# Output projection of six batches as three fp32r terms, with a per-tile split and single-buffered exponentials, in an RWKV + MoE layer

## The chip, the cores and the metric

The kernel runs on one core of one Trainium2 chip. The time is the device time of one launch in microseconds (us); less is better. Five engines work side by side: TensorE (PE, with its weight load PEld), VectorE (DVE), ScalarE (ACT), GpSimd (POOL) and the DMA queue that SyncE (SP) issues.

## The reference

For x of 8 batches x 512 steps x 512 channels (float32):

```python
shifted = pad(x)[:, :-1]
k = (x*mk + shifted*(1-mk)) @ Wk;  v = (... mv) @ Wv;  r = sigmoid((... mr) @ Wr)
# per channel, over time: a decaying, max-stabilised softmax average of v under weights exp(k)
out_t = (e1*num + e2*v_t) / (e1*den + e2);  num, den, mx updated with the decay
x = layernorm(x + (r * out) @ Wo)                   # the "output projection" is @ Wo
x = layernorm(x + moe(x))                           # 8 experts of 16 units, top 2, silu
```

## The kernel before

Channels lie on the 128 partitions in C = 4 chunks, time on the free axis. The unit of the recurrence is one chunk of one batch, 128 channels x 512 steps, U = 32 units. Every engine runs the same hand-written loop over **slots** s = 0..31; slot s works on unit u = s of batch b = s // 4, and j = s % 4 is its place in the batch. No scheduler moves anything: each engine does its list in program order and waits on semaphores.

In slot s:

- TensorE computes the key of unit s+1 (`key`, PSUM bank PK0 or PK1), the receptance of unit s (`rec`, bank PR) and the value of unit s+1 (`value`, bank PV). From batch 1 on each is a `split`: weights and inputs are stored as a high part (rounded to fp32r) and a low part (the rest), and every product is three fp32r matmuls (high x high, high x low, low x high), 12 per unit. Batch 0 uses plain fp32 (`whole`).
- VectorE runs the recurrence: `scan_den`, `value_kept`, `scan_num`, `value_now`, `numerator`, then `scan_max` and `lead` for unit s+1, `gate`, `weigh`. `weigh` writes r * out of the unit to a ring RW. It also makes the token-shift mixes of the next batch (`mix`: 4 chunks for each of key, value, receptance; it reads D and XT, both in SBUF), and the two residuals.
- ScalarE forms the exponentials (`decay_gates`: three Relus; `decay_exps`: three Exps, both into EX), the sigmoid chain on PR (`receptance`, `log_g`, `factor`), the high parts of the mixes (`highs`) and the layernorm spreads.
- GpSimd forms the denominators (`denominator`: DQ from DEN and EX), the low parts of the mixes (`lows`: mix minus high part; KL in slots j = 2, VL and RL in slots j = 3), the layernorm scaling (`normalise`), and in slots j = 0 the four differences D of the next batch.

The ring through the engines in one slot is: `lead` (DVE) -> `decay_gates` (ACT) -> `log_g`, `factor` (ACT) -> `weigh` (DVE) -> ... -> `scan_den` of the next slot. `gate` (DVE) has to be done before `log_g`, and it waits for the receptance's Exps.

The output projection of a batch runs four slots later: tile t (128 time steps) in slot t + 4 for t < 24 and two tiles in each of slots 28 and 29. It is `project(t)`: four fp32 matmuls of 512 columns into bank PP, stationary operand 128 x 128 columns of RW, moving operand WO. In slots j = 0 it stands before `rec`, else after `rec` and the transposes `turn`. The last four tiles (28 to 31) are done in the tail.

Buffers that matter here: EX is two buffers (EX[u % 2]), RW a ring of 8 units, KT four separate mix buffers, SCR a scratch of 4 chunks that holds the key mixes of batch 0 and the throw-away output of the layernorm squares. Wk, Wv and Wr are staged in X1T, XN0 and XN1, then split into high and low parts in slots 0 to 2; a low part of 128x2048 is made on VectorE for Wk (`WKL`) and on GpSimd for Wv and Wr (`WVL`, `WRL`).

Of the kernel before, what the change touches and what calls it, by code (L numbers as in the profile page):

```python
# [23 lines left out]
NRW = 8  # L24
# [5 lines left out]
def rwkv_moe_postln(nc, x, xt, vec, wk, wv, wr, wo, dr, up, tri, out):  # L30
    with ExitStack() as ctx:
# [13 lines left out]
        WO = sb("WO", [128, C, H])  # L45
# [10 lines left out]
        KT = [sb(f"KT{i}", [128, T]) for i in range(NKT)]  # L56
# [52 lines left out]
        class Part:  # L109
            def __init__(self, k):  # L110
# [7 lines left out]
                self.s1, self.s2 = (x[:, i, EI * lo:EI * hi] for i in range(2))  # L118
                self.gt, self.eq = (x[:, 2 if tail else 1, o + E * E * lo:o + E * E * hi] for o in (0, 256))
# [82 lines left out]
        def _(eng):  # L202
# [66 lines left out]
        def _(eng):  # L269
# [844 lines left out]
```

## Time and profile before

| | |
|---|---|
| time, 3 runs | 499.42 us median (499.01 to 499.54) |
| the profiled execution | 498.65 us, its span 496.8 us |
| PE busy | 471.4 us (95%) |
| DVE busy | 409.2 us (82%) |
| ACT busy | 339.9 us (68%) |
| POOL busy | 259.7 us (52%) |
| granted TensorE clock | 0.99 of full speed over the span |

A batch repeats every 57.4 us from batch 3 on: the `scan_den` of slots 17 to 21 start at 247.09, 260.31, 273.63, 290.21 and 304.45 us. Busy time of an engine says how full it is, not whether anybody waits for it; for that the timelines show in brackets the idle time before an instruction and what ended it. "x4" in a timeline row means four instructions merged, and an fp32 matmul of 512 columns appears as two records.

### The profile page before, as it was taken

The page shows a single profiled execution, that of the slowest core. Times are in us where ns is not written, and L with a number is a line of the kernel's source. Part 1 is how long each engine was busy: PE and PEld are TensorE (multiplying, and loading weights), DVE is VectorE, ACT ScalarE, POOL GpSimd, SP SyncE. Part 2 cuts the span into 40 slices and gives each one's busy share as a digit, 9 for nine tenths or more (in the row PEclk, how much of TensorE's full clock was granted, in tenths as well). Part 3 has the DMA queues.
Part 4 walks back from the last instruction along what each step waited for, and adds up shares of the span by engine and source line. Part 5 has one row for each costly group of instructions (what it writes and reads, how often), then busy time and mean ns, then how long its engine had stood idle before and what let it go on. Part 6 is the DMA issues. An engine that isn't in the chain of part 4 may idle for free. (4 is left out here: it accounts for less than half of the span.)

```text
span 496.8 us, 6301 instructions
## 1 busy us (share of the span) xinstructions
PE 471.4 (95%) x1850; PEld 315.1 (63%) x1850; DVE 409.2 (82%) x655; ACT 339.9 (68%) x769; POOL 259.7 (52%) x279
## 2 busy tenths in 40 slices
PE   8998799999999999999999999999999998989991
PEld 3444367776776666766867666776767666756550
DVE  6998988897799869997799887997799977755686
ACT  1568465766877587777877768776877776936574
POOL 2446763666425973556815965358625664021226
PEclk9999899999999999999999999999999999999997
DMA  9800340002000232003210043003120013300005
GB/s 249 275 8 5 126 146 1 0 11 77 1 1 0 72 99 85 1 1 128 74 53 1 22 128 106 0 1 114 58 84 1 0 43 107 106 0 2 1 35 220
DMA packets 20098, 30.35 MB, mean 61 GB/s; under 512 B 2016, under 2 KB 7136, under 8 KB 20064
## 3 DMA queue, kind: packets, MB, share of 16 engines
q1 hardware_dynamic: 20064, 29.95, 18.6%
q8 instruction: 15, 0.25, 0.2%
q14 instruction: 19, 0.16, 0.1%
HBM read 21.56 MB, written 8.39 MB: 60 GB/s over the span
## 5 line engine op out<-in xcount | busy, mean ns | idle before, releaser
L506 ACT ACTIVATE PR<-PR 128x512 f32<-128x512 f32 x128 | 74.4, 581 | 51.0 <-PE PR L294 24.7
L318 PE MATMUL PP<-WO,RW 128*128 128x512 f32 x232 | 104.6, 593 | 1.6 <-DVE XN L783 1.6
L1016 POOL TENSOR_SCALAR NM<-SUM,RS 128x1 f32<-128x1 f32 x30 | 8.4, 280 | 145.0 <-ACT RS L506 145.0
L318 PEld LDWEIGHTS PP<-WO,RW 128*128 128x128 f32 x232 | 42.4, 190 | 46.1 <-issue 43.5
L1010 POOL TENSOR_TENSOR DQ<-DEN,EX 128x512 f32<-128x512 f32 x32 | 41.2, 1286 | 37.6 <-DVE DEN L720 37.6
L757 DVE TENSOR_TENSOR RW<-NU,PR 128x512 f32<-128x512 f32 x32 | 22.0, 688 | 42.1 <-ACT PR L506 42.0
L768 DVE SCALAR_TENSOR_TENSOR KT<-D,VEC,XT 128x512 f32<-128x512 f32 x56 | 52.1, 961 | 0.0
L290 PE MATMUL PR<-RH,WRH 128*128 128x512 f32 x112 | 48.8, 436 | 0.0
L290 PE MATMUL PK<-KH,WKH 128*128 128x512 f32 x112 | 47.6, 425 | 0.0
L290 PE MATMUL PV<-VH,WVH 128*128 128x512 f32 x112 | 46.4, 414 | 1.2 <-DVE NU L744 1.2
L506 ACT ACTIVATE EX<-PK 128x512 f32<-128x512 f32 x32 | 19.1, 596 | 41.1 <-DVE PK L713 41.1
L720 DVE TENSOR_TENSOR_SCAN DEN<-PK,EX 128x512 f32<-128x512 f32 x32 | 39.1, 1221 | 9.1 <-ACT EX L506 7.5
L1003 POOL TENSOR_TENSOR RL<-D,RH 128x512 fp32r<-128x512 f32 x28 | 39.2, 1411 | 14.1 <-ACT RH L506 14.1
L294 PE MATMUL PV<-VL,WVH 128*128 128x512 f32 x112 | 44.0, 393 | 0.1
L294 PE MATMUL PR<-RL,WRH 128*128 128x512 f32 x112 | 44.1, 394 | 0.0
L294 PE MATMUL PK<-KL,WKH 128*128 128x512 f32 x112 | 44.0, 393 | 0.0
L291 PE MATMUL PV<-VH,WVL 128*128 128x512 f32 x112 | 43.8, 391 | 0.0
L291 PE MATMUL PR<-RH,WRL 128*128 128x512 f32 x112 | 43.7, 390 | 0.0
L291 PE MATMUL PK<-KH,WKL 128*128 128x512 f32 x112 | 43.7, 390 | 0.0
L506 ACT ACTIVATE SCR<-XN,SUM 128x512 f32<-128x512 f32 x53 | 37.8, 713 | 7.3 <-DVE XN L783 7.3
L707 DVE TENSOR_TENSOR_SCAN M<-CST,PK 128x512 f32<-128x512 f32 x32 | 38.9, 1217 | 2.9 <-PE PK L294 2.5
L737 DVE TENSOR_TENSOR_SCAN NUM<-PK,EX 128x512 f32<-128x512 f32 x32 | 39.2, 1225 | 1.1
(196 smaller groups left out, 1108.6 us busy)
## 6 DMA issues: line engine op xcount, KB each, us to landing
XT<-in_xt SPq DMA_DIRECT2D x32, 256.0 KB, 3.3
XN<-in_x SPq DMA_DIRECT2D x28, 256.0 KB, 2.6
out<-XN SPq DMA_DIRECT2D x28, 256.0 KB, 2.0
WO<-in_wo SPq DMA_DIRECT2D x1, 1024.0 KB, 7.7
XT<-in_x SPq DMA_DIRECT2D x4, 256.0 KB, 4.3
out<-XT SPq DMA_DIRECT2D x4, 256.0 KB, 2.2
X1T<-in_wk SPq DMA_DIRECT2D x2, 256.0 KB, 4.9
XN<-in_wv SPq DMA_DIRECT2D x2, 256.0 KB, 5.2
```

Of the source, the lines that this page charges most:

```text
L290: eng.matmul(dst[:, :], wh[:, c, o], high[:, c, :], start=(c == 0), stop=False)
L291: eng.matmul(dst[:, :], wl[:, c, o], high[:, c, :], start=False, stop=False)
L294: last = eng.matmul(dst[:, :], wh[:, c, o], low[:, c, :], start=False, stop=(c == C - 1))
L318: last = eng.matmul(projected_at(t), RW[(C * b + c) % NRW][:, 128 * n:128 * n + 128], WO[:, c, :], start=(c == 0), stop=(c == C - 1))
L506: eng.activation(*a, **k).then_inc(q[s], 1)
L707: eng.tensor_tensor_scan(M[:, 1:T + 1], TD[:, j:j + 1].to_broadcast([128, T]), PK[u % 2][:, :], NEG, ALU.add, ALU.max).then_inc(q["m"], 1)
L720: eng.tensor_tensor_scan(DEN[:, 1:T + 1], PK[u % 2][:, :], EX[u % 2][:, 0, :], 0.0, ALU.mult, ALU.add)\
L737: eng.tensor_tensor_scan(NUM[:, 1:T + 1], PK[u % 2][:, :], EX[u % 2][:, 0, :], 0.0, ALU.mult, ALU.add)\
L757: eng.tensor_tensor(RW[u % NRW][:, :], NU[:, :], PR[:, :], ALU.mult).then_inc(q["rw"], 1)
L768: eng.scalar_tensor_tensor(out=full(b, which, c), in0=D[:, c, :], scalar=VEC[:, 2 + which, c:c + 1], in1=XT[:, c, 0:T], op0=ALU.mult, op1= ...
L1003: eng.tensor_tensor(lo[:, c, :], full(b, which, c), hi[:, c, :].bitcast(F32), ALU.subtract)\
L1010: eng.tensor_tensor(DQ[:, :], DEN[:, 0:T], EX[u % 2][:, 1, :], ALU.add).then_inc(q["e"], 1)
```

## The change

- **WO becomes WOH and WOL.** Wo is loaded into X1T once the split of Wk (`lwk`) and all keys of batch 0 (`k` >= 4) are done; ScalarE makes WOH at the end of slot 2, GpSimd makes WOL (128x2048) in slot 3 between VL and RL. X1T is free for its own use after that (`turned(0)` waits for it).
- **`project(t)` for t < 24** is 12 fp32r matmuls from TH, TL, WOH, WOL, and now always stands after `rec` and `turn`. Tiles 24 to 31 stay fp32; their Wo is loaded again, into KT, in the SP list of batch 6.
- **`halve(t)`** on ScalarE copies the tile's four 128-column pieces of RW to TH at the end of slot t + 3, before `spread`; **`low_of_tile(t)`** on GpSimd writes TL = RW - TH in the same slot, before `normalise`. TH and TL are single buffers. Where the four units wrap around the ring (batches 1, 3, 5) each is two instructions.
- **EX is one buffer.** `decay_gates(u)` now waits for `num`, `bb` and `e` of unit u - 1 (was u - 2); `e` is GpSimd's `denominator`.
- **RW is a ring of 7**, `weigh` waits for `tl` instead of `wo_`. SCR is gone: the key mixes of batch 0 lie in RW[2], DR, JUNK and KT[3], its value mixes in RW[3] to RW[6], its receptance mixes in AGT, UP, HS0 and HS1. Therefore `mix(1, 0, 3)`, which writes KT[3] in slot 1, waits for all four keys of batch 0.

```diff
-NRW = 8
+NRW = 7
...
-        WO = sb("WO", [128, C, H])
+        WOH, WOL = sb("WOH", [128, C, H], F32R), sb("WOL", [128, C, H], F32R)
...
-        KT = [sb(f"KT{i}", [128, T]) for i in range(NKT)]
+        KT = sb("KT", [128, NKT, T])
...
-        EX = [sb(f"EX{i}", [128, 2, T]) for i in range(2)]
+        EX = sb("EX", [128, 2, T])
...
-        SCR = sb("SCR", [128, C, T])
-        RW = [sb(f"RW{i}", [128, T]) for i in range(NRW)]
+        JUNK = sb("JUNK", [128, T])
+        RW = sb("RW", [128, NRW, T])
+        TH, TL = sb("TH", [128, C, 128], F32R), sb("TL", [128, C, 128], F32R)
...
+        SPLIT = NT * (LAST - 1)
+
+        def pieces(b):
+            i = C * b % NRW
+            m = min(C, NRW - i)
+            return [(0, m, i)] + ([(m, C, 0)] if m < C else [])
...
-            load_w(WO, wo, "wo")
+            eng.wait_ge(q["lwk"], 1)
+            eng.wait_ge(q["k"], C)
+            load_w(X1T, wo, "wo")
...
+                if b == LAST - 1:
+                    eng.wait_ge(q["lo"], 3 * C * (LAST - 1) + 2 * C)
+                    load_w(KT, wo, "wot")
...
+                eng.wait_ge(q["th"], halved(t + 1))
+                for c in range(C):
+                    eng.matmul(PP[:, :], TH[:, c, :], WOH[:, c, :], start=(c == 0), stop=False)
+                    eng.matmul(PP[:, :], TH[:, c, :], WOL[:, c, :], start=False, stop=False)
+                eng.wait_ge(q["tl"], halved(t + 1))
+                for c in range(C):
+                    last = eng.matmul(PP[:, :], TL[:, c, :], WOH[:, c, :], start=False, stop=(c == C - 1))
+                last.then_inc(q["wo_"], 1)
...
-                if j == 0:
-                    for t in now[:1]:
-                        project(t)
                 rec(s)
...
-                if u >= 2:
-                    eng.wait_ge(q["num"], u - 1)
-                    eng.wait_ge(q["bb"], u - 1)
-                    eng.wait_ge(q["e"], u - 1)
+                if u:
+                    eng.wait_ge(q["num"], u)
+                    eng.wait_ge(q["bb"], u)
+                    eng.wait_ge(q["e"], u)
...
+            def halve(t):
+                b, n = divmod(t, NT)
+                eng.wait_ge(q["rw"], C * (b + 1))
+                if t:
+                    eng.wait_ge(q["wo_"], t)
+                for lo, hi, i in pieces(b):
+                    act("th", TH[:, lo:hi, :], RW[:, i:i + hi - lo, 128 * n:128 * n + 128], ACT.Copy)
...
+                if b == 1 and which == 0 and c == 3:
+                    eng.wait_ge(q["k"], C)
...
+            def low_of_tile(t):
+                b, n = divmod(t, NT)
+                for i, (lo, hi, k) in enumerate(pieces(b)):
+                    eng.wait_ge(q["th"], halved(t) + i + 1)
+                    eng.tensor_tensor(TL[:, lo:hi, :], RW[:, k:k + hi - lo, 128 * n:128 * n + 128],
+                                      TH[:, lo:hi, :].bitcast(F32), ALU.subtract).then_inc(q["tl"], 1)
```

On TensorE in slot 20 (batch 5, j = 0; the same in every slot j = 0), before, the projection PP stands between `ffn_up` (PU) and the receptance PR:

```order
L422 MATMUL PU<-UP,AGT 128x512 [waits s_res2,s_agc]
L318 MATMUL PP<-WO,RW 128x512 [waits s_res,s_rw]
L318 MATMUL PP<-WO,RW 128x512 x3
L290 MATMUL PR<-RH,WRH 128x512 [waits s_hi,s_rw]
L291 MATMUL PR<-RH,WRL 128x512
L294 MATMUL PR<-RL,WRH 128x512 [waits s_lo]
```

and of the change, from the end of the receptance of that slot on:

```order
L306 MATMUL PR<-RH,WRH 128x512 [waits s_hi]
L307 MATMUL PR<-RH,WRL 128x512
L310 MATMUL PR<-RL,WRH 128x512 [waits s_lo]
L390 MATMUL PT<-IDN,XN 128x128 [waits s_nrp,s_x1t]
L390 MATMUL PT<-IDN,XN 128x128 x3
L352 MATMUL PP<-WOH,TH 128x512 [waits s_th,s_res]
L353 MATMUL PP<-WOL,TH 128x512
```

The receptance has moved ahead of the projection, and the projection has to wait for TH and TL.

On GpSimd from slot 3 to slot 5, before (DQ is `denominator`, VL and RL are `lows`, D the differences, NM and XN the two instructions of `normalise`):

```order
L1003 TENSOR_TENSOR VL<-KT,VH 128x512 [waits s_hi] x4
L1003 TENSOR_TENSOR RL<-D,RH 128x512 [waits s_hi] x4
L1010 TENSOR_TENSOR DQ<-DEN,EX 128x512 [waits s_g,s_eq,s_den]
L997 TENSOR_TENSOR D<-XT 128x512 [waits s_lo,s_xt0]
L997 TENSOR_TENSOR D<-XT 128x512 [waits s_lo,s_xt1]
L997 TENSOR_TENSOR D<-XT 128x512 [waits s_lo,s_xt2]
L997 TENSOR_TENSOR D<-XT 128x512 [waits s_lo,s_xt3]
L1016 TENSOR_SCALAR NM<-SUM,RS 128x1 [waits s_rs1]
```

and of the change:

```order
L1048 TENSOR_TENSOR VL<-KT,VH 128x512 [waits s_hi] x4
L1123 TENSOR_TENSOR WOL<-X1T,WOH 128x2048 [waits s_woh]
L1048 TENSOR_TENSOR RL<-D,RH 128x512 [waits s_hi] x4
L1095 TENSOR_TENSOR TL<-RW,TH 128x512 [waits s_th]
L1055 TENSOR_TENSOR DQ<-DEN,EX 128x512 [waits s_g,s_eq,s_den]
L1042 TENSOR_TENSOR D<-XT 128x512 [waits s_lo,s_xt0]
L1042 TENSOR_TENSOR D<-XT 128x512 [waits s_lo,s_xt1]
L1042 TENSOR_TENSOR D<-XT 128x512 [waits s_lo,s_xt2]
L1042 TENSOR_TENSOR D<-XT 128x512 [waits s_lo,s_xt3]
L1095 TENSOR_TENSOR TL<-RW,TH 128x512 [waits s_th]
L1061 TENSOR_SCALAR NM<-SUM,RS 128x1 [waits s_rs1]
```

WOL has come in between VL and RL, and one TL ahead of each `normalise`.

On VectorE in slot 1, the change makes the fourth key mix of batch 1, which stands between `gate` and `weigh`, wait for the keys (s_k):

```order
L813 SCALAR_TENSOR_TENSOR KT<-D,VEC,XT 128x512 [waits s_d] x3
L788 SCALAR_TENSOR_TENSOR PR<-PR,DQ 128x512 [waits s_t,s_e]
L813 SCALAR_TENSOR_TENSOR KT<-D,VEC,XT 128x512 [waits s_k,s_d]
L800 TENSOR_TENSOR RW<-NU,PR 128x512 [waits s_c,s_f]
L759 SCALAR_TENSOR_TENSOR DEN<-PK,EX 128x512 [waits s_e,s_ea,s_eb]
```

Before, that mix had no wait but the one for D, at the same place.

## Rows read from the trace of the kernel before

**Rows 1.** One batch in the windows view: us; busy of PE, PEld, DVE, ACT, POOL; clock.

```profile
245.00:302.40 57.40, 56.73 (x238) 40.14 (x237) 48.96 (x78) 42.89 (x100) 33.60 (x36) 1.00 0.17 56
```

**Rows 2.** Timeline of VectorE, slots 18 and 19: start us, us, engine, instruction.

```profile
266.79 2.49 DVE L768 SCALAR_TENSOR_TENSOR KT<-D,VEC,XT 128x512 f32<-128x512 f32 x2
...
271.15 0.69 DVE L757 TENSOR_TENSOR RW<-NU,PR 128x512 f32<-128x512 f32 x1 [0.61 <-ACT PR L506]
...
280.72 1.96 DVE L768 SCALAR_TENSOR_TENSOR D<-D,VEC,XT 128x512 f32<-128x512 f32 x2
```

**Rows 3.** Timeline of VectorE, ScalarE and GpSimd in slot 20 (j = 0).

```profile
295.50 1.30 POOL L1010 TENSOR_TENSOR DQ<-DEN,EX 128x512 f32<-128x512 f32 x1
...
296.54 1.20 ACT L506 ACTIVATE PR<-PR 128x512 f32<-128x512 f32 x2 [2.17 <-PE PR L294]
296.63 0.76 DVE L713 SCALAR_TENSOR_TENSOR PK<-PK,CST,M 128x512 f32<-128x512 f32 x1
...
298.12 0.60 ACT L506 ACTIVATE EX<-PK 128x512 f32<-128x512 f32 x1
...
300.92 0.69 DVE L757 TENSOR_TENSOR RW<-NU,PR 128x512 f32<-128x512 f32 x1 [2.39 <-ACT PR L506]
```

**Rows 4.** Timeline of TensorE in slot 14: first of 12 split matmuls, transposes, projection, next.

```profile
202.08 0.39 PE L290 MATMUL PR<-RH,WRH 128*128 128x512 f32 x1
...
204.83 0.60 PE L398 MATMUL PU<-IDN,X1T 128*128 128x128 f32 x4
...
205.70 3.60 PE L318 MATMUL PP<-WO,RW 128*128 128x512 f32 x8
209.13 1.09 PE L381 MATMUL PH<-DR,X1T 128*128 128x136 f32 x8
```

**Rows 5.** Timeline of ScalarE (first row) and GpSimd, slots 14, 18 and 19.

```profile
203.19 2.18 ACT L506 ACTIVATE KH<-KT 128x512 fp32r<-128x512 f32 x4
...
260.75 0.26 POOL L1016 TENSOR_SCALAR NM<-SUM,RS 128x1 f32<-128x1 f32 x1 [10.55 <-ACT RS L506]
...
263.09 4.98 POOL L1003 TENSOR_TENSOR KL<-KT,KH 128x512 fp32r<-128x512 f32 x4
...
276.49 4.97 POOL L1003 TENSOR_TENSOR VL<-KT,VH 128x512 fp32r<-128x512 f32 x4
```

**Rows 6.** Timeline of TensorE and VectorE at the end of slot 1.

```profile
36.08 3.60 PE L276 MATMUL PK<-SCR,X1T 128*128 128x512 f32 x8
...
37.34 0.74 DVE L768 SCALAR_TENSOR_TENSOR KT<-D,VEC,XT 128x512 f32<-128x512 f32 x1
...
39.77 1.23 DVE L720 TENSOR_TENSOR_SCAN DEN<-PK,EX 128x512 f32<-128x512 f32 x1 [0.39 <-ACT PK L506]
```

**Rows 7.** Timeline of GpSimd and VectorE in slots 1 and 2.

```profile
30.38 4.57 POOL L1043 TENSOR_TENSOR WVL<-XN,WVH 128x2048 fp32r<-128x2048 f32 x1
...
46.84 6.31 DVE L768 SCALAR_TENSOR_TENSOR KT<-D,VEC,XT 128x512 f32<-128x512 f32 x2
47.53 5.07 POOL L1043 TENSOR_TENSOR WRL<-XN,WRH 128x2048 fp32r<-128x2048 f32 x1
```

**Rows 8.** Timeline of GpSimd and VectorE in slot 3.

```profile
57.52 5.00 POOL L1003 TENSOR_TENSOR VL<-KT,VH 128x512 fp32r<-128x512 f32 x4
62.06 2.33 DVE L768 SCALAR_TENSOR_TENSOR D<-D,VEC,XT 128x512 f32<-128x512 f32 x3
```

**Rows 9.** Timeline of VectorE and ScalarE in slot 4.

```profile
71.45 0.76 DVE L713 SCALAR_TENSOR_TENSOR PK<-PK,CST,M 128x512 f32<-128x512 f32 x1
72.11 1.20 ACT L506 ACTIVATE PR<-PR 128x512 f32<-128x512 f32 x2 [4.12 <-PE PR L294]
73.22 0.59 ACT L506 ACTIVATE EX<-PK 128x512 f32<-128x512 f32 x1
```

**Rows 10.** Timeline of TensorE in slots 2 and 3, across a gap.

```profile
39.51 1.05 PE L276 MATMUL PR<-AGT,XN 128*128 128x512 f32 x2
...
53.80 2.07 PE L276 MATMUL PR<-AGT,XN 128*128 128x512 f32 x2 [2.87 <-DVE RW L757]
```

More of the change, by code:

```diff
@@ L81, in rwkv_moe_postln @@
         TD, NTD, CC, QB = (CST[:, i, :] for i in range(4))
-        JUNK = SCR[:, 3, :]
         def full(b, which, c):
             if b == 0:
-                early = [AGT[:, :], UP[:, :]] + [h[:, :, :].rearrange("p n h -> p (n h)")[:, 0:T] for h in HS]
-                return (SCR[:, c, :], RW[C + c][:, :], early[c])[which]
+                flat = [h[:, :, :].rearrange("p n h -> p (n h)")[:, 0:T] for h in (DR, *HS)]
+                return ((RW[:, 2, :], flat[0], JUNK[:, :], KT[:, 3, :]), [RW[:, 3 + i, :] for i in range(C)],
+                        (AGT[:, :], UP[:, :], flat[1], flat[2]))[which][c]
             if which == 2:
                 return D[:, c, :]
-            return KT[(C * (2 * (b - 1) + which) + c) % NKT][:, :]
+            return KT[:, (C * (2 * (b - 1) + which) + c) % NKT, :]
         def xn_at(t):
@@ L117, in __init__ @@
                 gm = spare[:, 768:780].rearrange("p (i n) -> p i n", i=3) if tail else GM
-                self.s1, self.s2 = (x[:, i, EI * lo:EI * hi] for i in range(2))
-                self.gt, self.eq = (x[:, 2 if tail else 1, o + E * E * lo:o + E * E * hi] for o in (0, 256))
+                s1, s2, pairs = (M, DEN, NUM) if tail else (X1T[:, 0, :], X1T[:, 1, :], X1T[:, 1, :])
+                self.s1, self.s2 = (a[:, EI * lo:EI * hi] for a in (s1, s2))
+                self.gt, self.eq = (pairs[:, o + E * E * lo:o + E * E * hi] for o in (0, 256))
                 self.hs = hs[:, lo:hi, :]
@@ L170, in hs_at, with halved @@
             return p.hs[:, t - p.tiles[0], :]
+        SPLIT = NT * (LAST - 1)
[3 more added lines that the diff above has]
+            return [(0, m, i)] + ([(m, C, 0)] if m < C else [])
+        def halved(t):
+            return sum(len(pieces(u // NT)) for u in range(min(t, SPLIT)))
         def sems(names):
@@ L317, in projected @@
                 for c in chunks:
-                    last = eng.matmul(projected_at(t), RW[(C * b + c) % NRW][:, 128 * n:128 * n + 128], WO[:, c, :],
+                    last = eng.matmul(projected_at(t), RW[:, (C * b + c) % NRW, 128 * n:128 * n + 128], KT[:, c, :],
                                       start=(c == 0), stop=(c == C - 1))
@@ L427, in _ @@
             for _ in range(5):
-                eng.matmul(PP[:, :], RW[0][:, 0:128], RW[0][:, :], start=True, stop=True)
+                eng.matmul(PP[:, :], RW[:, 0, 0:128], RW[:, 0, :], start=True, stop=True)
             key(0)
@@ L449, in _ @@
                     turn(t)
-                for t in now[:1] if j else []:
+                for t in now[:1]:
                     project(t)
@@ L663, in _ @@
                     high_weights(s + 1)
+                if s == 2:
+                    eng.wait_ge(q["wo"], 16)
+                    act("woh", WOH[:, :, :], X1T[:, :, :], ACT.Copy)
                 for t in past[:1]:
@@ L669, in _ @@
                     spread2(t2 + 1)
+                if s == 3:
+                    highs(1, 2)
+                if C - 1 <= s < SPLIT + C - 1:
+                    halve(s - C + 1)
                 for t in now[:1]:
                     spread(t)
-                if s == 3:
-                    highs(1, 2)
                 for t in past[1:] if s < U - 2 else []:
@@ L755, in weigh @@
                 if u >= NRW:
-                    eng.wait_ge(q["wo_"], NT * ((u - NRW) // C + 1))
-                eng.tensor_tensor(RW[u % NRW][:, :], NU[:, :], PR[:, :], ALU.mult).then_inc(q["rw"], 1)
+                    over = NT * ((u - NRW) // C + 1)
+                    if over > SPLIT:
+                        eng.wait_ge(q["wo_"], over)
+                    else:
+                        eng.wait_ge(q["tl"], halved(over))
+                eng.tensor_tensor(RW[:, u % NRW, :], NU[:, :], PR[:, :], ALU.mult).then_inc(q["rw"], 1)
             def mix(b, which, c):
@@ L1068, in _ @@
                     normalise2(t2)
+                if s == 3:
+                    eng.wait_ge(q["woh"], 1)
+                    eng.tensor_tensor(WOL[:, :, :], X1T[:, :, :], WOH[:, :, :].bitcast(F32), ALU.subtract)\
+                       .then_inc(q["wol"], 1)
                 if j == 3 and batch(b + 1):
                     lows(b + 1, 2)
+                if C - 1 <= s < SPLIT + C - 1:
+                    low_of_tile(s - C + 1)
                 for t in now[:1]:
```

38 lines of the change are left out of this document (21 added, 17 removed), and 2 rows, old and new, of the table q.

## The prediction

> **What bounds the kernel now.** The page's first part says TensorE, 95% busy, and in one batch of the steady stretch it is busy for 56.73 of 57.40 us against 48.96 on VectorE [rows 1]. That says that TensorE is full; it does not say that anyone waits for it. So I then read VectorE's timeline through one batch, gap by gap, and asked of each gap what ended it. In slot 18 (j = 2) VectorE has one gap of any size, 0.61 us ahead of `weigh`, for ScalarE's `factor` [rows 2], and that is the latency of `gate` -> `log_g` -> `factor`; TensorE does not appear. Slot 17 looks the same, and in slot 19 the gaps again go to ScalarE, which itself waits for VectorE's mixes. In slot 20 (j = 0) TensorE does appear: ScalarE waits 2.17 us for the receptance, so `decay_gates` starts at 298.12 although `lead` ended at 297.39 (296.63 + 0.76), and VectorE then waits 2.39 us ahead of `weigh` [rows 3]. Hence two limits of nearly equal length lie side by side: TensorE's list, and the ring VectorE -> ScalarE -> VectorE. The ring sets the pace in three slots of four; TensorE costs it 0.7 us in the fourth (298.12 - 297.39). The reader should see that shortening TensorE's list is worth about 0.7 us a batch, and that anything that lengthens the ring counts in full.
>
> GpSimd comes into the ring through a side door. In slot 18 the first mix of VectorE, issued at 266.79, meets the last KL (KL runs from 263.09 to 268.07), and the two mixes take 2.49 us [rows 2, 5], where one alone takes 0.74 [rows 6]. In slot 2 two mixes take 6.31 us while GpSimd makes WRL, 5.07 us [rows 7]. So a VectorE instruction with both inputs in SBUF stands still for a whole GpSimd instruction. The Trainium skill ("SBUF — State Buffer", "Who interferes with whom") states this as an exclusive lock on a shared port pair, held for the whole instruction, against operands shared at half speed. By a half-speed rule two mixes of 0.74 beside WOL would take twice their time, so that the WOL term below would be about 1.5 us and not 4.6, and the sum 3 us less; the 6.31 us row agrees with the lock.
>
> **The change, part by part.**
>
> *TensorE.* Twelve fp32r matmuls take 2.75 us (202.08 to 204.83), the fp32 projection 3.43 (205.70 to 209.13) [rows 4]: 0.68 less per tile, some 0.1 of it lost at one more change of kind, so 24 x 0.58 = 14 us of TensorE time. What of it reaches the ring is only the j = 0 term: the receptance, now ahead of the projection, ends over 3 us earlier, and `decay_gates` can start at `lead`'s end: -0.65 us in each of slots 12, 16, 20, 24 and 28. In slot 8 the trace shows the receptance in time already, and slot 4 is counted below. Slots 28 to 31 keep their fp32 projections; the reload of Wo into KT is issued when slot 27's VL is done and needed a slot later, so I cost it at nothing (covered by the rest of slot 27 on all engines).
>
> *Start: the wait for the keys in slot 1.* `mix(1, 0, 3)` ran at 37.34; the fourth key runs from 36.08 for 3.60 [rows 6]. The mix now starts at 39.75, ends at 40.4, `weigh` (0.69) follows and `scan_den` starts at 41.0 instead of 39.77 [rows 6]: **+1.25** for all that follows; the ring through slot 2 has nothing that takes it up.
>
> *Start: WOL.* It is a 128x2048 subtraction like WVL, 4.57 us when alone [rows 7], and starts when VL ends, at 62.52 (57.52 + 5.00). VectorE's three D mixes start at 62.06 [rows 8]. As in slot 2, the first gets through and the second waits for all of WOL: +4.6. GpSimd next has RL waiting (1.25 each, as KL: 4.98 / 4 [rows 5]) and the two engines alternate, so the third mix waits for one RL, +1.2, and the fourth for part of one, +0.6. `scan_den(4)` starts 1.25 + 6.4 = **7.65 us** late. Nothing hides it: `weigh(3)` and all of the ring are queued behind those mixes. Of this 0.95 comes back in slot 4, where `decay_gates` started at 73.22 for lack of the receptance and could have started at 72.2 (71.45 + 0.76) [rows 9]. Left: **+6.7**.
>
> *Every tile: `halve` and `low_of_tile`.* `halve` costs ScalarE 0.55 us (four copies in 2.18 [rows 5]), 0.7 where it is two instructions. It stands after the Exps that `scan_den` needs, in time that ScalarE has idle, but ahead of `spread`, for which `normalise` waits (10.55 us idle, ended by RS [rows 5]). `low_of_tile` costs 1.28 us, as one KL (1.25 [rows 5]) or DQ (1.30 [rows 3]) does, ahead of `normalise`. So `normalise`, DQ and then KL start 0.57 us later, up to 0.95 where TL must first wait for a mix or `silu` on VectorE. What is late next is the meeting of KL and the mixes: KL ends that much later, the second mix stands behind it, then `gate`, `log_g`, `factor`, `weigh`. I take 0.8 in slots 6, 10, 14, 18, 22, 26: **+4.8**. In slots j = 3 VL (276.49 to 281.46) meets the D mixes (280.72, 1.96 us for two [rows 2, 5]) in the same way; 0.6 in slots 7 to 27: **+3.6**. Both ends: nothing, if the meetings fall out kindly, and 1.25 (a whole KL) in each, 15 us.
>
> *Slots j = 0, tail.* TL itself meets the three key mixes in slots 4 and 8, where no second spread stands between: 0.65 to 1.3 each, **+1.5**. In slots 12 to 24 the mixes move 0.65 us forward and so onto a `normalise2` of GpSimd that they used to follow; I take the gain there as lost (+0.65 each against -0.65), and keep it in slot 28 alone, which has no mixes: **-0.6**.
>
> *EX single-buffered.* The new wait is for `e` of the same ring turn. In slot 20 DQ ends at 296.80 against `lead` at 297.39 [rows 3]: 0.6 of slack, and GpSimd will be 0.65 later there. It costs 0 to 0.2 us a batch, and nothing in the other slots, where DQ ends as KL starts, at 263.09, and the mixes, behind `lead`, start only at 266.79 [rows 2, 5]. RW of 7 and the waits for `tl` cost nothing: the writer comes half a slot after.
>
> **Sum:** 6.7 + 4.8 + 3.6 + 1.5 - 0.6 = +16.0 us on the profiled execution's 498.65 (span 496.8 and 1.85 around it, which does not change): 514.65; the median of the runs is 0.77 above that execution, so **515.4 us**.
>
> **Rivals.**
>
> 1. *The start alone* (20%). The steady terms are differences of half a microsecond between two engines that meet by chance; they may cancel, and then the -0.65 of the slots j = 0 stays as well: 499.4 + 8.2 (6.7 + 1.5) - 5 x 0.65 = 504 us, or 507.6 if the latter is lost. For it: the slots from 12 on have TensorE's slack now. Against it: in slots j = 2 and 3 KL and VL are later by what stands in front of them, and the mixes are not.
>
> 2. *TensorE is the bound after all* (9%), the other side. All 14 us arrive and the start costs the same 8.2: 493.6 us; with the start hidden too, 485. For it: 56.73 of 57.40 us busy [rows 1] and every batch alike. It decides if VectorE's gaps in slots j = 1 to 3 are set by TensorE in some way the releasers don't show. Against it: there, the 0.61 us gap is ScalarE's two instructions and no more.
>
> 3. *The clock falls* (10%). TensorE now has some 4 us more of idle a batch (4 x 0.58 saved, 1.4 from the longer batch), and most of it collects ahead of `ffn_up` in slots j = 0, where it waits for VectorE: up to 3 us in one piece. After the one gap of that size in this trace, 2.87 us, two records took 2.07 us instead of 1.05 [rows 10], the lower of the two levels (1.2 against 2.4 GHz). Then the receptance of each slot j = 0 takes 2.7 us more, which about uses up the 3 us by which it has become earlier, and slot 28 loses 1.2 and not gains: 515.4 + 6 x 0.6 + 1.8 = 521 us. The Trainium skill ("TensorE: Matmul & The Clock Gate", "HAM oscillation") says that gaps in which the engine idles bring it back to half rate, and by it this rival would be the likeliest; the gaps here are mostly shorter than that of rows 10.
>
> 4. *EX holds the ring* (6%). If `normalise` and `normalise2` push DQ of slots j = 0 by a whole TL more (1.28), `decay_gates` starts 1 us late in six slots: 521 us.
>
> **Range and chances.** The likeliest case (55%) spans 510 to 520 on its own: the steady terms between 4 and 13 us. With rival 1 below and the 521 us of rivals 3 and 4 above, 503 to 521.5 us holds 8 in 10. Faster by more than 0.2% (about 1 us, what a measurement of this kernel can tell from no change) has 9%, within it 3%, slower 88%.
>
> **What the profile of the changed kernel would show.** Slot 1: a gap of about 1.7 us ahead of the fourth KT mix, ended by TensorE's keys. Slot 3: three D mixes of 8 us or more beside a WOL of 4.6 to 5.1, and `scan_den(4)` near 73 us. Steady: a batch of 58 to 59 us instead of 57.4, TensorE below 93% in it with its gaps ahead of `ffn_up` in slots j = 0; KL two mixes of 3.1 us instead of 2.49; in slots j = 0 `decay_gates` right behind `lead`. I am wrong if the batch is 57 us or shorter (rival 1 or 2), if the D mixes of slot 3 stay under 3 us, or if the clock of the steady stretch is below 0.97 (rival 3).

## The result, and the profile after

| | before | changed |
|---|---|---|
| median, 4 runs each on one chip | 499.22 us | 512.45 us (511.45 to 513.88) |
| ratio | | 1.0269, 95% interval 1.024 to 1.0299 |
| the profiled execution, its span | 498.65, 496.8 us | 511.88, 509.5 us |

The change makes the kernel 13.2 us slower. (Two of the eleven executions of experiment 4, 574 and 608 us at a granted clock of 0.85 and 0.75 over the whole run, are left out of every number below.) First the page of the changed kernel, its first part (busy time, share of the span, instructions), and the window of one steady batch, which answers to [rows 1]:

```profile
PE 462.4 (91%) x1946; PEld 334.6 (66%) x1946; DVE 425.4 (83%) x655; ACT 355.9 (70%) x806; POOL 305.7 (60%) x316
```

```profile
254.80:313.00 58.20, 54.46 (x253) 42.78 (x253) 50.70 (x78) 45.22 (x105) 40.75 (x44) 1.00 0.17 55
```

TensorE is busy for 9 us less in all, and in a batch 3.7 us without work where it had 0.7; the batch still grew from 57.4 to 58.2 us. GpSimd is the engine that grew, by 46 us.

Where the time went is read from the starts of `scan_den`, one in each slot, in both traces. The differences between successive ones, in us:

| place | predicted | measured |
|---|---|---|
| slot 1, wait for the keys | +1.25 | +1.29 |
| slots 2 and 3 (WOL) | +6.4 | +5.36 (-0.31 and +5.67) |
| slots 4 and 8 | -0.95 + 1.5 | +0.08 and +0.23 |
| slots j = 2, six | 6 x 0.8 | 0.61, 0.80, 0.66, 0.79, 0.63, 0.78: +4.3 |
| slots j = 3, six | 6 x 0.6 | 0.65, 0.47, 0.44, 0.45, 0.60, 0.44: +3.1 |
| slots 12, 16, 20, 24 | 0 | -0.30, -0.24, -0.30, -0.25: -1.1 |
| slot 28 to the end | -0.6 | +0.02 in slots 28 and 29, -0.26 in slot 30, -0.05 behind it |

Their sum is +12.9; the changed kernel's first slot began 0.19 us earlier, which gives the 12.7 us between the spans.

VectorE in slots 1 and 3 of the changed kernel, with the wait for the keys and the D mixes (it answers to [rows 6, 8]):

```profile
39.60 0.75 DVE L813 SCALAR_TENSOR_TENSOR KT<-D,VEC,XT 128x512 f32<-128x512 f32 x1 [2.33 <-PE PK L292]
...
62.85 7.66 DVE L813 SCALAR_TENSOR_TENSOR D<-D,VEC,XT 128x512 f32<-128x512 f32 x3
70.44 0.68 DVE L800 TENSOR_TENSOR RW<-NU,PR 128x512 f32<-128x512 f32 x1
71.03 1.16 DVE L813 SCALAR_TENSOR_TENSOR D<-D,VEC,XT 128x512 f32<-128x512 f32 x1
72.11 1.21 DVE L759 TENSOR_TENSOR_SCAN DEN<-PK,EX 128x512 f32<-128x512 f32 x1
```

and GpSimd beside it in slot 3:

```profile
58.30 4.99 POOL L1048 TENSOR_TENSOR VL<-KT,VH 128x512 fp32r<-128x512 f32 x4
63.26 5.03 POOL L1123 TENSOR_TENSOR WOL<-X1T,WOH 128x2048 fp32r<-128x2048 f32 x1
68.25 6.31 POOL L1048 TENSOR_TENSOR RL<-D,RH 128x512 fp32r<-128x512 f32 x4
74.52 1.28 POOL L1095 TENSOR_TENSOR TL<-RW,TH 128x512 fp32r<-128x512 f32 x1
```

Three mixes that cost 2.33 us in [rows 8] take 7.66: one of them stands for WOL from 63.26 to 68.29. RL, 5.0 us alone, takes 6.31, so GpSimd waits for VectorE as well.

The steady slots j = 2 and 3 of the changed kernel, GpSimd and VectorE (it answers to [rows 2, 5]):

```profile
269.69 1.85 POOL L1095 TENSOR_TENSOR TL<-RW,TH 128x256 fp32r<-128x256 f32 x2 [8.17 <-ACT TH L530]
271.53 0.25 POOL L1061 TENSOR_SCALAR NM<-SUM,RS 128x1 f32<-128x1 f32 x1
...
273.86 5.49 POOL L1048 TENSOR_TENSOR KL<-KT,KH 128x512 fp32r<-128x512 f32 x4
...
276.62 3.28 DVE L813 SCALAR_TENSOR_TENSOR KT<-D,VEC,XT 128x512 f32<-128x512 f32 x2
...
287.71 5.50 POOL L1048 TENSOR_TENSOR VL<-KT,VH 128x512 fp32r<-128x512 f32 x4
...
291.34 2.43 DVE L813 SCALAR_TENSOR_TENSOR D<-D,VEC,XT 128x512 f32<-128x512 f32 x2
```

KL starts 3.71 us behind `scan_den` (270.15) where it was 2.78 (263.09 - 260.31), and the two mixes take 3.28 us where they took 2.49. The mixes themselves are issued at the same distance from `scan_den`, 6.47 us and 6.48: only what they meet has moved.

Slot 20, j = 0, ScalarE and VectorE (it answers to [rows 3]):

```profile
308.55 0.60 ACT L530 ACTIVATE EX<-PK 128x512 f32<-128x512 f32 x1 [0.99 <-DVE PK L752]
...
311.34 0.69 DVE L800 TENSOR_TENSOR RW<-NU,PR 128x512 f32<-128x512 f32 x1 [2.17 <-ACT PR L530]
...
312.56 2.43 DVE L813 SCALAR_TENSOR_TENSOR KT<-D,VEC,XT 128x512 f32<-128x512 f32 x3
```

`decay_gates` stands right behind `lead` (end 308.47) and not behind the receptance. `weigh` comes 10.05 us behind `scan_den` (301.29), where it was 10.71. TensorE's new idle time stands in these slots:

```profile
306.21 0.63 PE L390 MATMUL PT<-IDN,XN 128*128 128x128 f32 x4 [2.08 <-POOL XN L1064]
```

It is 2.08 us ahead of `turn`, for GpSimd's `normalise`, and another 1.19 us ahead of `ffn_up` (300.29).

### The profile page after: what moved, and what is told of

Read it like the earlier page. It is cut to its first block and busy times, and to the rows that moved or that the text cites. A ratio compares the mean times of both kernels' runs of the same rounds, so it can differ in the third digit from the quotient of the medians.

```text
span 509.5 us, 6617 instructions
## 1 busy us (share of the span) xinstructions
PE 462.4 (91%) x1946; PEld 334.6 (66%) x1946; DVE 425.4 (83%) x655; ACT 355.9 (70%) x806; POOL 305.7 (60%) x316
## 5 line engine op out<-in xcount | busy, mean ns | idle before, releaser
L1095 POOL TENSOR_TENSOR TL<-RW,TH 128x512 fp32r<-128x512 f32 (+3 forms) x36 | 34.5, 973 | 93.2 <-ACT TH L530 93.2
L813 DVE SCALAR_TENSOR_TENSOR KT<-D,VEC,XT 128x512 f32<-128x512 f32 x57 | 59.3, 1071 | 2.3 <-PE PK L292 2.3
L530 ACT ACTIVATE JUNK<-XN,SUM 128x512 f32<-128x512 f32 x53 | 37.8, 713 | 7.3 <-DVE XN L828 7.3
L530 ACT ACTIVATE RH<-D 128x512 fp32r<-128x512 f32 x28 | 17.6, 629 | 34.9 <-DVE D L813 34.9
L352 PE MATMUL PP<-WOH,TH 128*128 128x512 f32 x96 | 40.7, 424 | 0.0
```

Source lines behind the costliest of these rows:

```text
L352: eng.matmul(PP[:, :], TH[:, c, :], WOH[:, c, :], start=(c == 0), stop=False)
L530: eng.activation(*a, **k).then_inc(q[s], 1)
L813: eng.scalar_tensor_tensor(out=full(b, which, c), in0=D[:, c, :], scalar=VEC[:, 2 + which, c:c + 1], in1=XT[:, c, 0:T], op0=ALU.mult, op1= ...
L1095: eng.tensor_tensor(TL[:, lo:hi, :], RW[:, k:k + hi - lo, 128 * n:128 * n + 128], TH[:, lo:hi, :].bitcast(F32), ALU.subtract).then_inc(q[" ...
```

## The experiments

The theory under test: the ring of VectorE and ScalarE sets the pace, GpSimd's instructions lengthen it where they meet VectorE's mixes, and TensorE costs it 0.7 us in a slot j = 0. The main rival: TensorE, the fullest engine, is the bound.

### 1. Half of the projection left out

```diff
 # before.py, project(t), t < 24
-                projected(t, range(C)).then_inc(q["wo_"], 1)
+                    for c in (0, 3):
+                        last = eng.matmul(projected_at(t), RW[...], WO[:, c, :], start=(c == 0), stop=(c == C - 1))
```

> The kernel before with two of the four fp32 matmuls of each projection of tiles 0 to 23 left out (chunks 1 and 2, so half of the sum is missing): 24 x 1.7 = 41 us less for TensorE, everything else as it is. Theory (the batches are bound by the ring of VectorE, ScalarE and the last product, and by VectorE's lists in j=2 and j=3; TensorE's time shows in j=0 alone): at most -0.7 us a batch, -3 to -5 us, 494.5 to 496.5 us. Rival (TensorE is the bound at 98.8 percent busy): -30 to -40 us, 460 to 470 us.

Measured: 498.1 us beside 498.7; ratio 0.9981 (0.9968 to 0.9993). 41 us less of TensorE's work (24 x 3.43 / 2; its busy time on the page falls by 30 us, from 471.4 to 441.0) gave 0.6 us. The slots j = 0 from 12 on each gave 0.43 to 0.44 us, where [rows 3] put 0.7, 1.7 in all, and one loss of 1.19 us in slot 6 took most of it away. Every other slot was the same to 0.04 us. The loss is worth a look. GpSimd and VectorE of this kernel in slot 6,

```profile
93.99 5.45 POOL L1009 TENSOR_TENSOR KL<-KT,KH 128x512 fp32r<-128x512 f32 x4
...
96.38 3.62 DVE L774 SCALAR_TENSOR_TENSOR KT<-D,VEC,XT 128x512 f32<-128x512 f32 x2
```

and of the kernel before:

```profile
93.94 5.92 POOL L1003 TENSOR_TENSOR KL<-KT,KH 128x512 fp32r<-128x512 f32 x4
...
96.29 2.42 DVE L768 SCALAR_TENSOR_TENSOR KT<-D,VEC,XT 128x512 f32<-128x512 f32 x2
```

With `scan_den` at 89.90 and 89.81, the mixes are issued 6.48 us behind it in both, KL 4.09 and 4.13. The two meetings differ by 0.04 us in their timing and by 1.2 us in their price, about the length of one KL. I read it so that a few hundredths of a microsecond decide which of the two engines gets in first; no run moves KL by that amount alone.

### 2. The order on TensorE alone

```diff
 # before.py, TensorE's loop
-                if j == 0:
-                    for t in now[:1]:
-                        project(t)
                 rec(s)
...
-                for t in now[:1] if j else []:
+                for t in now[:1]:
                     project(t)
```

> The kernel before with only the new order on TensorE: in slots j=0 the projection of the tile stands behind the receptance matmuls instead of ahead of them; it stays in fp32. Theory (the receptance product is on the ring of j=0, so it comes 3.4 us earlier, but TensorE's list is itself nearly full there and the ring of j=0 can shrink only by its idle time): -0.3 to -0.65 us in each of six or seven batches, 495 to 497.5 us. Rival (TensorE bounds the batch, order moves nothing): 499 to 499.5 us.

Measured: 498.35 us; ratio 0.9983 (0.9974 to 0.9991). Real, but less than half of the least that was expected: slots 12, 16, 20 and 24 gave 0.47 to 0.49 us each, slot 30 0.23, slots 8 and 28 nothing, and slot 6 lost 1.2 us as in experiment 1, here 1.0 by the meeting (two KT mixes in 3.42 us) and 0.2 because VectorE first waits 0.34 us for TensorE's value. Expected were six or seven slots and no loss.

### 3. The wait for the keys alone

```diff
 # before.py, mix
+                if b == 1 and which == 0 and c == 3:
+                    eng.wait_ge(q["k"], C)
```

> The kernel before with one added wait: the last key mix of batch 1, in slot 1, waits until all four key products of batch 0 are done, as in the changed kernel. Theory: the mix comes 1.25 us later and scan_den(2) with it, of which slot 3 takes back 0.3: +0.8 to +1.2 us, 500.0 to 500.4 us. Rival (the start's later slots have slack that takes all of it back): 499.2 us.

Measured: 499.66 us beside 499.05; ratio 1.0022 (1.0009 to 1.0035). In the trace `scan_den(2)` is 1.28 us late and slot 2 gives 0.32 back, as in the changed kernel. The runs fell into two groups, seven of 499.1 to 499.7 and five of 500.4 to 501.9 us, and the profiled one is of the second (501.9); its first slot also began 0.84 us later than in the profile of the kernel before. The first group lies only 0.3 us above the kernel before, so in it most of the wait is taken back; no trace shows where. The profiled execution has a loss of 1.16 us in slot 4 that the changed kernel has not. ScalarE in slot 4 of this kernel (it answers to [rows 9], where the wait is 4.12 us):

```profile
75.08 1.20 ACT L506 ACTIVATE PR<-PR 128x512 f32<-128x512 f32 x2 [5.29 <-PE PR L294]
```

So it is TensorE that is late. Windows of this kernel,

```profile
60.00:62.00 2.00, 0.51 (x2) 0.45 (x3) 1.91 (x4) 0.54 (x1) 2.00 (x3) 0.95 0.83 221
62.00:64.00 2.00, 2.00 (x7) 1.51 (x6) 1.97 (x4) 0.61 (x2) 2.00 (x2) 0.50 0.97 344
64.00:66.00 2.00, 2.00 (x8) 1.59 (x7) 2.00 (x3) 1.97 (x4) 0.28 (x1) 0.70 0.40 112
```

and of the kernel before:

```profile
62.00:64.00 2.00, 1.91 (x9) 1.25 (x8) 2.00 (x4) 1.97 (x5) 0.52 (x1) 1.00 0.79 290
```

After a stretch with little work on TensorE the granted clock falls to 0.50 (1.2 GHz) here at 62 us and in the kernel before at 53, where nobody waits. The kernels of experiments 4 and 6 have the dip at 59 to 63 us and lost 1.1 to 1.3 us in slot 4 too; those of experiments 1, 2, 8 and 9 have it at 53 to 58 us and lost nothing there. That this explains the second group of runs is argued from the profiles, not tested.

### 4. One buffer of exponentials alone

```diff
 # before.py
-        EX = [sb(f"EX{i}", [128, 2, T]) for i in range(2)]
+        EX = [sb("EX", [128, 2, T])] * 2
...
-                if u >= 2:
-                    eng.wait_ge(q["num"], u - 1)
+                if u:
+                    eng.wait_ge(q["num"], u)          # bb and e likewise
```

> The kernel before with one buffer of exponentials in place of two, and the waits on the slot's own numerator scan, product and denominator that this needs, nothing else. Theory (the writer is released by then in every slot): 0 to +0.2 us a batch, 499.2 to 500.5 us. Rival (it holds the ring of each slot by 0.15 to 0.2 us): +5 us, 504 us.

Measured: 499.44 us beside 499.05; ratio 1.0004 (0.9995 to 1.0013): the same within the interval, and no slot after the fourth differs by more than 0.02 us from the one of before. Slot 4 of this execution is 1.11 us longer, by the wait for the receptance (5.23 us against 4.12 [rows 9]) and the later dip of the clock that experiment 3 shows, not by the buffer. The writer is released in time as long as GpSimd's list is that of the kernel before.

### 5. The split alone, with nothing that uses it

```diff
 # before.py with experiment 4, TH, TL and RW as one tensor
+                act("th", TH[:, :, :], RW[:, i:i + C, 128 * n:128 * n + 128], ACT.Copy)     # ScalarE, before spread; highs(1, 2) ahead of it
...
+                eng.tensor_tensor(TL[:, :, :], RW[...], TH[:, :, :].bitcast(F32), ALU.subtract)  # GpSimd, before normalise
```

> The kernel before, with the single buffer of exponentials and the two instructions of the split of each of the tiles 0 to 23 (ScalarE copies the four weighted chunks of a tile to fp32r, GpSimd forms the rest), while TensorE still multiplies in fp32 and nothing uses the split: no term of the start, no gain on TensorE. Theory (the 1.42 us of GpSimd work a tile sit in the handover from GpSimd to the mixes and tiles' highs in slots j=2 and j=3, +0.8 and +0.6 a batch for six batches, and nothing in j=0 and j=1): +7 to +9 us, 506.5 to 508.5 us. Rival (the split is hidden and the after kernel's growth in the batches comes from the new order and timing of TensorE's matmuls): 499 to 501 us. Rival (a single buffer of exponentials holds the ring): the kernel with that alone, run beside this one, shows most of it.

Measured: 508.96 us beside 499.05; ratio 1.0198 (1.0185 to 1.0211). 9.9 us for instructions that take, in a slot of 14 us, 1.3 us on GpSimd and 0.6 on ScalarE, which were 52% and 68% busy. Slots j = 2 from 6 on gave +0.54 to +0.61, slots j = 3 +0.55 to +0.59, in all 12 slots 6.9 us; the rest came in slots 4 (+1.98) and 8 (+1.03) and in slots 12, 16, 20 and 24 (+0.13 each). In slot 8 TL meets the key mixes (three in 3.12 us against 2.07); in slot 4 it does too, and the other 0.9 us is the single buffer of exponentials, as ScalarE shows:

```profile
74.20 0.60 ACT L507 ACTIVATE EX<-PK 128x512 f32<-128x512 f32 x1 [0.75 <-POOL DQ L1022]
```

`decay_gates` starts 8.49 us behind `scan_den` and not 7.57, since TL has pushed DQ back. In slots j = 2 and 3 this is most of the changed kernel's growth (7.3 us), with no change on TensorE at all.

### 6. ScalarE's half of the split, and GpSimd's

```diff
 # the kernel of experiment 5; first run
-                    low_of_tile(s - C + 1)
 # second run: no copy, TL = RW - RW
-                    halve(s - C + 1)
```

> The kernel of the split alone (fp32 projection kept, split unused) with GpSimd's subtractions left out: ScalarE's 24 copies to TH remain. Theory (ScalarE has time in every slot, what costs is GpSimd's handover to the mixes): 0 to +0.15 us a batch beyond the single buffer, 499.0 to 500.5 us. Rival (the copy lies between a slot's exponentials and the next slot's work on ScalarE and is itself on the ring): +0.6 us a slot j=2 or j=3, 505 to 509 us.

> The kernel of the split alone with ScalarE's copies left out: GpSimd's 24 subtractions of a tile's shape remain (of the chunks from themselves, with the wait for the weighted values and none for a copy). Theory: nearly all of the split's cost is theirs, 506 to 509 us, +0.6 in slots j=2 and j=3. If they can run earlier, since they wait for no copy, they may end ahead of the key rests and cost less: what is then missing from the +9.9 us of the split alone is the copy's delay of them, not the copy's own time. Rival (GpSimd's work hides, the copies cost): 499 to 500.5 us.

Measured: the copy alone 504.41 us, ratio 1.0109 (1.0094 to 1.0124); the subtraction alone 503.76, ratio 1.0098 (1.0084 to 1.0113), beside 498.92. My theory fell: I had taken the copy for hidden, and it costs 5.5 us, the subtraction 4.8. Of the totals in their traces, 6.1 and 5.0 us, slot 4 has 1.1 and 1.3, which experiment 4 has as well by the clock; the rest, 5.0 and 3.7, is theirs. (RW - RW is also shorter than the real TL, 1.04 us against 1.28.) The copy costs 0.29 to 0.45 in each slot j = 2 and 0.46 to 0.51 in each slot j = 3. GpSimd and VectorE in slot 19 of the kernel with the copy alone:

```profile
281.12 4.96 POOL L1015 TENSOR_TENSOR VL<-KT,VH 128x512 fp32r<-128x512 f32 x4
...
284.86 2.44 DVE L780 SCALAR_TENSOR_TENSOR D<-D,VEC,XT 128x512 f32<-128x512 f32 x2
```

VL starts 3.34 us behind `scan_den` (277.78) and in the kernel before 2.86 (276.49 - 273.63 [rows 5]); GpSimd does nothing more than before, but `normalise` waits for the spread, the spread for the copy, and VL stands behind `normalise`. So 0.52 us on ScalarE, in time it has idle, becomes 0.48 us later for VL and 0.48 us longer for the mixes (2.44 against 1.96). The subtraction alone waits for no copy and runs as soon as GpSimd's list comes to it: in slots j = 3 behind the last RL, where no mix stands, and these slots cost nothing; in slots j = 2 right behind KL, where from slot 10 on it catches the second mix (3.27 us for two) and costs 0.76 to 0.78. The two costs are of different meetings, and that they add up to that of both together is partly chance.

The rule that the kernels with the copy follow, slots 18 and 19, start of KL or VL and time of the two mixes, both against the kernel before (in all 12 slots KL or VL starts 0.48 to 0.97 us later and the slot is 0.29 to 0.80 us longer):

| | KL later | mixes longer | VL later | mixes longer |
|---|---|---|---|---|
| copy alone | 0.51 | 0.30 | 0.48 | 0.48 |
| split alone | 0.80 | 0.58 | 0.58 | 0.62 |
| changed kernel | 0.93 | 0.79 | 0.59 | 0.47 |

### 7. WOL at another place

```diff
 # after.py, GpSimd's list, the WOL subtraction
+ behind low_weights(2), ahead of lows(b + 1, 1)
- behind lows(b + 1, 1), ahead of lows(b + 1, 2)
```

> The changed kernel with one move: the subtraction that forms WOL stands on GpSimd behind the start's weights for the receptance in slot 2's list, ahead of the value rests of slot 3, in place of between the value rests and the receptance rests. Theory (in slot 3 the 5 us of WOL block three receptance mixes on VectorE for their length, which delays the ring's slot 4 by 5.7 us; earlier, WOL meets less of VectorE's work with its own shape and the later rests come in shape for it): 3 to 5 us less than the changed kernel, 507.5 to 509.5 us, with scan_den(4) at 67 to 69 us. Rival (any place for WOL costs the same 5 us, since GpSimd's list itself is the start's bound): 511.5 to 512.5 us.

Measured: 509.8 us beside 498.7, just above the expected 507.5 to 509.5; ratio 1.0224 (1.021 to 1.0238), so some 2.2 to 2.7 us less than the changed kernel. GpSimd in slot 3:

```profile
58.90 4.52 POOL L1119 TENSOR_TENSOR WOL<-X1T,WOH 128x2048 fp32r<-128x2048 f32 x1
63.37 6.34 POOL L1048 TENSOR_TENSOR VL<-KT,VH 128x512 fp32r<-128x512 f32 x4
```

WOL itself now meets no mix (4.52 us, its length alone), but VL, 4.5 us later, meets the D mixes in its place: three in 5.12 us where they took 7.66. `scan_den(4)` starts at 70.19 and not 72.11; the expected 67 to 69 was too low, since the mixes now wait for VL in place of WOL. Slot 4 costs 1.1 us here, beside a granted clock of 0.50 from 62 to 70 us; by slot 8 the trace is 1.9 us ahead of the changed kernel's and stays so.

### 8. The gate first

```diff
 # before.py, VectorE's loop
+                if j == 2:
+                    gate(s)
                 if j == 2 and b:
                     mixes(b + 1, 1, 0, 1)
...
-                gate(s)
+                if j != 2:
+                    gate(s)
```

> The kernel before with one move on VectorE: in slots j=2 the gate (PR times DQ) stands ahead of the first two key mixes in place of behind them. Theory (ScalarE waits 1.3 to 2 us for the gate there while its exponentials for the next slot wait behind it, and VectorE waits 0.2 to 0.6 us for the weighted value's factor; the mixes wait for nothing new): -0.5 to -0.9 us in each of seven j=2 slots, 493.5 to 496 us. Rival (VectorE's list is full in j=2 and holds the next scan whatever the order): 499 us.

Measured: **494.55 us** beside 498.7; ratio 0.9917 (0.9903 to 0.993). This beats both kernels. Slots 10, 14, 18, 22 and 26 gave 1.29 to 1.30 us each, more than the 0.5 to 0.9 expected, but slots 16, 20, 24 and 28 took 0.69 to 0.74 back. ScalarE in slot 20:

```profile
294.04 1.20 ACT L506 ACTIVATE PR<-PR 128x512 f32<-128x512 f32 x2 [2.86 <-PE PR L294]
...
295.62 0.60 ACT L506 ACTIVATE EX<-PK 128x512 f32<-128x512 f32 x1
```

The wait for the receptance rose from 2.17 [rows 3] to 2.86 us and `decay_gates` starts 1.42 us behind `lead` (end 294.20). The window of one batch says why:

```profile
245.32:301.95 56.63, 56.30 (x238) 40.29 (x237) 48.12 (x79) 42.74 (x99) 33.67 (x37) 1.00 0.18 56
```

TensorE idles 0.33 us in it. Here it is the bound, now that the ring is shorter.

### 9. Gate first, and what TensorE then is worth

```diff
 # before.py: first run = experiments 8 + 2; second run = experiments 8 + 1
```

> The kernel before with both moves: the gate first in slots j=2 on VectorE, the projection behind the receptance matmuls in slots j=0 on TensorE. Theory (the two act in different slots, and the order alone gave -0.48 us in each of four slots j=0, less one loss of 1.2 us in slot 6): their sum, -4 to -7 us, 492.5 to 495.5 us. Rival (TensorE is so full that what one gives the other can not keep): no better than the gate alone.

> The kernel before with the gate first in slots j=2 and two of the four projection matmuls of tiles 0 to 23 left out (chunks 1 and 2, half of the sum missing). Theory (with the gate first the batch of the kernel before has come down to TensorE's own 56.7 us, which is why slots j=0 gave 0.7 us back; with 41 us less work there they do not): each batch of seven keeps 1.3 us and the 0.43 us of the halved projection, -10 to -12 us on before, 486.5 to 489 us. Rival (slots j=0 give back 0.7 us because of VectorE's and ScalarE's own lists): 493.5 to 494.5 us, as with the gate first alone.

Measured: with the order 495.25 us, ratio 0.9933 (0.992 to 0.9945), no better than the gate alone: the rival's answer. Slots j = 0 from 12 on gave their 0.48 us and slots j = 3 0.26, but slots j = 2 from 14 on only 0.12 in place of 1.3: TensorE's list is full and the time comes out elsewhere, 0.86 us a batch against 0.72 with the gate alone; slot 6 lost 0.67 us and the gate alone gained 0.11 there. With half of the projection left out 489.97 us, ratio 0.9815 (0.98 to 0.983), and the window of about a batch (`scan_den` of slots 17 and 21 start at 243.66 and 299.13, 55.47 us apart):

```profile
243.70:299.20 55.50, 51.17 (x222) 36.69 (x220) 48.27 (x79) 42.74 (x99) 33.95 (x37) 1.00 0.18 57
```

Slots j = 0 give 0.42 us in place of taking 0.7, so the giving back was TensorE's. The same 41 us of its work that were worth 0.6 us in experiment 1 are worth 4.8 us here (9.0 against 4.2 us, each beside its own runs of the kernel before). The expected 10 to 12 us on before came as 9.0: slot 6 gained 0.1 and not 1.3.

### 10. The changed kernel with both improvements

```diff
 # after.py: experiments 7 + 8
```

> The changed kernel with WOL ahead of the value rests and with the gate first on VectorE in slots j=2. Theory (TensorE has 0.7 us a tile to spare in this kernel, so each of seven slots j=2 keeps the 1.3 us that the gate's move gave there in the kernel before, and slots j=0 do not take 0.7 us back): -7 to -9 us on the 509.8 us of the kernel with the early WOL alone, 501 to 503 us. Rival (the split's instructions on GpSimd hold the slot anyway): -4 us or less, 506 us or more.

Measured: 502.7 us beside 498.92; ratio 1.0075 (1.0062 to 1.0088), 7.1 us under experiment 7. From slot 10 on slots j = 2 gained 0.4 to 1.3 on that kernel and slots j = 3 0.4 to 0.7; slot 8 lost 1.1. In slot 20 TensorE's clock fell to 0.50 from 301.5 to 304.9 us, behind a gap of 2.07 us, and that slot was 0.3 us longer than slots 12, 16 and 24. The gap of 8.2 us to the gate alone is the start, some 4 us of it by slot 6, and the split.

## Why the prediction was right

The forecast was 515.4 us in a range of 503.0 to 521.5, the result 512.45. Its mechanism held, and the terms are 3 us too large in sum. The largest misses are -1.1 us each in slots 12 to 24 and in the split, +0.6 in slot 28, and one agreement, that of experiment 5 with the sum of the split's terms, is luck.

- **The ring, not TensorE, is the bound** was right: experiment 1. "About 0.7 us a batch" for TensorE measured 0.45.
- **The wait for the keys**: +1.25 predicted, +1.29 measured, and +1.28 in the trace with the wait alone, of whose runs the median is 0.6 us longer. The gap ahead of the mix was foreseen as 1.7 us and is 2.33; by the prediction's own times it would have been 2.4 (39.75 - 37.34). "The ring through slot 2 has nothing that takes it up" was wrong by the 0.3 us that came back there.
- **WOL**: +6.4 predicted, +5.67 measured in slot 3. The 5.8 of the first three mixes (4.6 for WOL and 1.2 for one RL) came as 5.33 (7.66 against 2.33 us), the 0.6 of the fourth as 0.4 (1.16 against 0.74 us).
- **"Of this 0.95 comes back in slot 4"** came about: `decay_gates` starts 6.60 us behind `scan_den` in place of 7.57. TL against the key mixes took 1.04 of it (3.11 us for three against 2.07) where I had 0.65. Windows of the changed kernel show what I had not foreseen: TensorE idled 4.57 us while the mixes stood, and ran the receptance of slot 4 at 0.50 of its clock (1.2 GHz). It was in time all the same, since the projection no longer stood ahead of it.

```profile
68.00:70.00 2.00, 0.00 (x0) 0.00 (x0) 2.00 (x2) 0.63 (x1) 2.00 (x3) 0.89 0.06 11
...
72.00:74.00 2.00, 2.00 (x6) 1.52 (x6) 1.90 (x3) 1.15 (x2) 2.00 (x2) 0.50 0.60 201
```

- **The split in slots j = 2 and 3**: 0.8 and 0.6 predicted, 0.71 and 0.51 on average measured (4.3 and 3.1 us in all). The path (copy, spread, `normalise`, DQ, KL or VL, mixes) is what experiments 5 and 6 show; the +0.48 us of VL with the copy alone is its plainest form. Experiment 5 makes the split alone cost 9.9 us. That is the prediction's own 4.8 + 3.6 + 1.5, but by chance: of the 10.4 us in its trace 6.9 are in slots j = 2 and 3, 3.0 in slots 4 and 8, a third of the latter by the wait for DQ, and 0.5 in slots 12 to 24.
- **Slots j = 0**: "I take the gain there as lost" was half right. `weigh` comes 0.66 us earlier; the three mixes meet `normalise2` (1.68 us in place of 0.78 for its second instruction) and take 2.43 us in place of 2.08: 0.35 of 0.66 is lost, -0.3 stays, which makes -1.1 us in four slots where the prediction had 0.
- **Slot 8**: TL against the key mixes was to cost 0.65 to 1.3 us and cost nothing; the three mixes took 2.07 us as before, and TL came behind them. The 0.23 us are of another cause, a small piece of rival 3. TensorE, ScalarE, VectorE and a window of the changed kernel in this slot:

```profile
131.02 1.08 PE L390 MATMUL PT<-IDN,XN 128*128 128x128 f32 x4 [2.98 <-POOL XN L1064]
...
139.75 0.28 ACT L530 ACTIVATE HS<-PH 128x136 f32<-128x136 f32 x1 [1.59 <-PE PH L408]
...
140.06 0.19 DVE L862 TENSOR_REDUCE GM<-HS 128x4 f32<-128x32 f32 x1
```

```profile
132.00:134.00 2.00, 2.00 (x6) 1.55 (x6) 1.97 (x3) 0.77 (x2) 2.00 (x3) 0.50 0.01 4
```

Behind a gap of 2.98 us TensorE ran at 0.50 from 131.0 to 134.4 us, and the tile's hidden copy came after the mixes' end (139.9) and not before it. By an estimate from these 3.4 us at half rate (1.7 us lost) it would have been in time at full clock.
- **Slot 28, -0.6**: the failed step. `weigh` is 0.69 us earlier, but the router's reduction right after it waits for the tile's hidden copy, 1.15 us where it was 0.44 (changed kernel, then the kernel before):

```profile
430.38 0.19 DVE L862 TENSOR_REDUCE GM<-HS 128x4 f32<-128x32 f32 x1 [1.15 <-ACT HS L530]
```

```profile
417.38 0.19 DVE L817 TENSOR_REDUCE GM<-HS 128x4 f32<-128x32 f32 x1 [0.44 <-ACT HS L506]
```

I had asked only whether mixes follow in that slot, not what TensorE's new order makes late: `hidden`, behind the projection. All of the gain went there (+0.01). The -0.26 us of slot 30 was not foreseen; the order alone (experiment 2) gives -0.23 there.
- **EX, RW, the second Wo** at nothing: 0.4 us with an interval that holds zero for EX (experiment 4). This is the buffer without the split. With TL ahead of DQ it did hold the ring (rival 4), by 0.9 us in slot 4 of experiment 5 and by some 0.05 us in slots 16 and 24 of the changed kernel, where `decay_gates` starts at DQ's end, 7.30 us behind `scan_den` and not 7.26. In slot 20 no slack is left: DQ ends at 308.44, `lead` at 308.47.
- **The rivals**: the start alone did not happen, nor TensorE as the bound. The clock stayed at 1.00 from slot 9 on until the tail with 3.7 us of idle in a batch, in gaps of up to 2.1 us, and the larger gap of each batch stands ahead of `turn`, not of `ffn_up` as rival 3 has it. TensorE was busy for 93.6% of the steady batch (54.46 of 58.20 us), just above the 93% that was named as a sign. The Trainium skill ("TensorE: Matmul & The Clock Gate", "HAM oscillation") tells of waits of several microseconds between bursts of matmuls, each of which brings half rate back. The changed kernel shows half rate at the start and in slot 8, behind gaps such as 4.57 and 2.98 us; the gaps of its steady batches are shorter than the section's, so by it rival 3 was not "the likeliest".
- By the lock of the Trainium skill ("SBUF — State Buffer", "Who interferes with whom") the mix caught by WOL stands for its whole length, and the trace agrees: 7.66 us against 2.33.

## What to carry to other kernels

An engine that is 95% or 99% busy is not the bound until someone is seen waiting for it; ask in each kind of slot what ends the last wait, and take work off that engine to see what it is worth (0.6 us of 41 here). Work put on engines with time to spare costs its delay to what is queued behind it there, through as many engines as it takes to reach the ring: 0.52 us on an idle ScalarE was 0.48 us on VectorE. Where two limits lie within a percent, shorten first the one that is waited for (moving the gate, 4.2 us) and only then the other.

## What the runs showed that was not expected

- The price of a meeting between GpSimd and VectorE jumps with its phase: 0.04 us of shift made the same two mixes take 3.62 in place of 2.42 us. In small comparisons such a step of 1.2 us can hide or feign an effect, as in experiments 1 and 2; compare slot by slot.
- At the start TensorE's granted clock falls to 0.50 in every kernel of this study, for 3.4 us in most, 7 us in experiment 5 and 10 us in all in the changed kernel and experiments 7 and 10. Before 59 us a dip of 3.4 us cost nothing, at 59 to 65 us some 1.1 us. The length of the gap does not settle it: a gap of 2.9 us at 51 to 54 us stands in the kernel before and in experiment 4 alike, and the clock fell there in the one, while in the other it held 1.00 until 59 us.
- GpSimd pays as well: RL took 6.31 us and VL 6.34 us for four, against 5.0 undisturbed.
